# An embedding tower unrolled, with three one-tile gather buffers and nine tables looked up by matmul

## The reference

```python
e = jnp.stack([tbl_f[ids[:, f]] for f in range(26)], axis=1)      # [B, 26, 128], written out in full
combined = jnp.concatenate([dense[:, None, :], e], axis=1)         # [B, 27, 128]
inter = jnp.einsum('bfd,bgd->bfg', combined, combined)[:, TRIU_I, TRIU_J]   # 351 pairs
z = jnp.concatenate([dense, inter], axis=1)
h = jnp.concatenate([z, dense], axis=1)                            # [B, 607]
h = relu(h @ W_top1 + b_top1)                                      # 512
h = relu(h @ W_top2 + b_top2)                                      # 256
y = h @ W_top3                                                     # 1
```

## Time and profile before

| | us |
|---|---|
| median of 3 runs | 683.96 (681.14 to 686.35) |
| span of the profiled execution | 696.8 |
| PE busy / POOL busy / DVE busy / ACT busy in it | 377.1 / 312.2 / 209.2 / 92.9 |
| granted TensorE clock in it, mean | 0.740 of full speed |

### The profile page before, as it was taken

The page is one execution under the profiler, slowest core; times in us unless marked ns, Lnnn a source line. Parts: engine busy times, 40 slices in busy tenths (PEclk is TensorE's granted clock), DMA queues, the critical chain, the costliest instruction groups (busy, mean ns, idle before and its releaser), DMA issues.

```text
span 696.8 us, 13458 instructions
## 1 busy us (share of the span) xinstructions
PE 377.1 (54%) x5828; PEld 317.6 (46%) x5828; DVE 209.2 (30%) x561; ACT 92.9 (13%) x159; POOL 312.2 (45%) x308
## 2 busy tenths in 40 slices
PE   1306523396284843927349082771817547194897
PEld 1306422394174732717238071561716545083875
DVE  3524007140083100921029010461006600075121
ACT  1111000021011200202002020100201011011132
POOL 6770546304537054470736617174271733637100
PEclk9757755598588775977769595695858858588798
DMA  5651111111101111030101201012010200101000
GB/s 163 189 159 61 41 38 47 31 54 37 41 15 53 64 42 34 21 104 4 49 26 29 100 12 53 16 38 87 20 53 8 98 26 27 49 7 52 19 3 2
DMA packets 18087, 34.32 MB, mean 49 GB/s; under 512 B 8241, under 2 KB 10929, under 8 KB 18065
## 3 DMA queue, kind: packets, MB, share of 16 engines
q0 software_dynamic: 9728, 19.94, 10.0%
q1 hardware_dynamic: 8338, 14.06, 6.1%
HBM read 33.97 MB, written 0.01 MB: 49 GB/s over the span
## 4 chain that ended last, share of the span: by engine, by line
PE 47%; issue 29%; another core or an unknown queue 16%; DMA 4%; ACT 3%; DVE 1%; SPq 0%; ACTq 0%
PE flip_ps L306 15%; PE gram_ps L323 12%; PE flip_ps L290 6%; PE mlp_ps L348 6%; PE mlp_ps L357 5%; DMA raw_then_y<-tbl 4%; ACT feats L456 2%; PE mlp_ps L350 2%; PE mlp_ps L376 1%; ACT hi L619 1%; PE pairs_ps L336 0%; ACT xT L546 0%; ACT xT L549 0%; DVE dots L468 0%
## 5 line engine op out<-in xcount | busy, mean ns | idle before, releaser
L269 POOL DMA_INDIRECT emb<-tbl,idx x304 | 312.0, 1026 | 336.4 <-DMA idx<-ids 225.5
L306 PE MATMUL flip_ps<-marks,hi 125*128 125x256 f32 x448 | 129.6, 321 | 106.0 <-ACT feats L456 102.0
L323 PE MATMUL gram_ps<-feats 128*27 128x27 f32 x4096 | 86.2, 202 | 169.2 <-issue 165.6
L448 DVE COPY feats<-flip_ps 128x512 f32<-128x512 f32 x56 | 38.5, 688 | 400.8 <-remote 247.9
L323 PEld LDWEIGHTS gram_ps<-feats 128*27 128x27 f32 x4096 | 63.7, 113 | 200.1 <-issue 198.6
L306 PEld LDWEIGHTS flip_ps<-marks,hi 125*128 125x128 f32 x448 | 98.8, 220 | 110.9 <-issue 69.7
L484 DVE TENSOR_SCALAR marks<-id_cols,row_no 125x256 fp32r<-125x256 int32 x448 | 127.5, 362 | 32.8 <-remote 25.1
L306 PE MATMUL flip_ps<-marks,lo 125*128 125x256 f32 x448 | 124.6, 310 | 0.9 <-issue 0.9
L306 PEld LDWEIGHTS flip_ps<-marks,lo 125*128 125x128 f32 x448 | 98.7, 220 | 2.1 <-issue 1.8
L290 PE MATMUL flip_ps<-ident,emb 128*128 128x128 f32 x320 | 62.2, 320 | 31.2 <-issue 18.2
L456 ACT COPY feats<-flip_ps 128x512 f32<-128x512 f32 (+1 forms) x32 | 31.5, 984 | 237.0 <-remote 126.1
(11 more groups left out here) (23 smaller groups left out, 77.9 us busy)
## 6 DMA issues: line engine op xcount, KB each, us to landing
id_cols<-ids_in_pairs SPq DMA_DIRECT2D x8, 896.0 KB
emb<-tbl,idx POOLq DMA_INDIRECT x304
emb<-dense SPq DMA_DIRECT2D x16, 64.0 KB
raw_then_y<-tbl SPq DMA_DIRECT2D x2, 500.0 KB
dots<-tbl SPq DMA_DIRECT2D x2, 500.0 KB
h1T<-tbl SPq DMA_DIRECT2D x2, 500.0 KB
w1p_sb<-w_pairs SPq DMA_DIRECT2D x1, 702.0 KB
w_sb<-w SPq DMA_DIRECT2D x1, 512.0 KB
```

The lines of the kernel that those rows point to most:

```text
L269: nc.gpsimd.indirect_dma_start(emb[:, u, f, :], None, tables[order[f - 1]][:, :], bass.IndirectOffsetOnAxis(ap=idx[:, u, order[f - 1]:orde ...
L306: last = nc.tensor.matmul(flip_ps[:, m % 2, 2 * (s % 2):2 * (s % 2) + 2, :], part[s][0:R[s], c, :], marks[0:R[s], s % MARK_SLOTS, c, :], s ...
L323: last = nc.tensor.matmul(gram_ps[QUAD * j:QUAD * j + F, n, 0:F], row, row, start=True, stop=True)
L448: copy(feats[:, u, :, GROUP * k:GROUP * k + n], flip_ps[:, m % 2, 0:n, :].rearrange("d f p -> d p f")).then_inc(s_kept[m % 2], 1)
```

## The change

- The loops go: the program is written out for all 16 tiles.
- `LOOKED_UP` goes from 7 to 9 (two tables of 1,250 rows, also cut into 125 rows or fewer for each chunk, join the seven), so 17 tables are gathered for each tile. Marks and look-ups are handed over in half tables (4 chunks), with four half-table mark slots in place of four whole ones.
- `emb` has three slots of one tile. The gathers of tile t wait for the flips of tile t-3. The third slot serves as two of the waiting places of the raw tables at the start (five places now), so the gathers of tile 2 wait until all nine tables are split (`s_lo`).
- All ids are loaded at the start in two DMAs; `id_cols` is double-buffered. Tiles are now 128 consecutive samples. Each tile's outputs are stored by a DMA of their own.
- PE's order: a look-up group comes ahead of its flip, the third layer ahead of `pair_rows`, and the gram of both tiles is in quarters. ACT makes `hi` with looked-up groups between. DVE copies all flips of tile 0, ACT all of tile 1.

```diff
-LOOKED_UP = 7
+LOOKED_UP = 9
+SLOTS = 3
...
-        idx = sb("idx", [P, 2, TABLES], i32)
-        emb = sb("emb", [P, 2, GATHERED, P])
+        idx = sb("idx", [P, tiles, TABLES], i32)
+        emb = sb("emb", [P, SLOTS, GATHERED * P])
-        marks = sb("marks", [P, MARK_SLOTS, MAX_CHUNKS, 2 * P], fp32r)
+        marks = sb("marks", [P, MARK_SLOTS, HALF_CHUNKS, 2 * P], fp32r)
...
# SP, after the loads of tables and weights
-            with sp.Fori(1, pairs) as i:
-                sp.wait_ge(s_marked, LOOKED_UP * i)
-                load_columns(i)
-                for u in range(2):
-                    sp.wait_ge(s_flip, GROUPS * (2 * (i - 1) + u + 1))
-                    load_idx(i, u)
-                    load_dense(i, u)
+            sp.wait_ge(s_lo, LOOKED_UP)
+            load_dense(2)
+            for t in range(SLOTS, tiles):
+                sp.wait_ge(s_flip, GROUPS * (t - SLOTS + 1))
+                load_dense(t)
+                i = t // 2
+                if t % 2 and i + 1 < pairs:
+                    sp.wait_ge(s_marked, 2 * LOOKED_UP * i)
+                    load_columns(i + 1)
+                if t % 2 and i >= 2:
+                    store(2 * (i - 2), i - 2)
+                    store(2 * (i - 2) + 1, i - 2)
...
# POOL
-                    pool.wait_ge(s_idx[u], 16 * i + 16)
-                    if not first:
-                        pool.wait_ge(s_flip, GROUPS * (2 * (i - 1) + u + 1))
+            for t in range(tiles):
+                v = t % SLOTS
+                if t < 2:
+                    pool.wait_ge(s_idx[t], 16)
+                if t == SLOTS - 1:
+                    pool.wait_ge(s_lo, LOOKED_UP)
+                if t >= SLOTS:
+                    pool.wait_ge(s_flip, GROUPS * (t - SLOTS + 1))
...
# PE
+            def looking_up(i):
+                for k in range(GROUPS):
+                    look_up(i, k)
+                    if i and k == 0:
+                        pair_rows(2 * i - 1)
+                    flip(2 * i, k)
+                    if i and k:
+                        first_layer(i - 1, BOTH, 2 * (i - 1), range(k - 1, k))
+            for i in range(pairs):
+                looking_up(i)
+                for part in range(4):
+                    gram(2 * i, part)
+                    if part < 3:
+                        flip(2 * i + 1, part)
+                if i:
+                    second_layer(i - 1, BOTH)
+                flip(2 * i + 1, 3)
+                if i:
+                    third_layer(i - 1, BOTH)
+                pair_rows(2 * i)
+                if i == pairs - 1:
+                    first_layer(*LAST[0], 2 * i)
+                flip(2 * i + 1, 4)
+                for part in range(4):
+                    gram(2 * i + 1, part)
...
# DVE
+            for i in range(pairs):
+                if i:
+                    lay_out(2 * i - 1)
+                    dve.wait_ge(s_xT, 2 * (2 * i - 2) + 1)
+                mark_table(i, 2)
+                keep(2 * i, 0)
+                mark_table(i, 3)
+                mark_table(i, 4)
+                keep(2 * i, 1)
+                mark_table(i, 5)
+                mark_table(i, 6)
+                keep(2 * i, 2)
+                mark_table(i, 7)
+                mark_table(i, 8)
+                keep(2 * i, 3)
+                keep(2 * i, 4)
...
+                if i + 1 < pairs:
+                    mark(i + 1, 0)
+                lay_out(2 * i)
+                if i + 1 < pairs:
+                    mark(i + 1, 1)
+                    mark_table(i + 1, 1)
...
# ACT, at the start
             for s in range(LOOKED_UP):
                 act.wait_ge(s_raw[s % PLACES], 16 * (s // PLACES + 1))
                 nc.scalar.copy(hi[s][0:R[s], :, :], waiting(s)).then_inc(s_hi, 1)
+                if s >= 4 and s % 2 == 0:
+                    keep_looked(0, s // 2 - 2)
```

## The result

The changed kernel took 721.96 us (718.81 to 724.28, 4 runs) against 682.55 us (678.57 to 686.35, 4 runs): 1.057 times as long, with an interval of 1.051 to 1.063. The forecast was 711, slower, within 655 to 733.

The account below looks back on a forecast made before the run. Bound: PE shut out during POOL's gather runs. Period 24.4 + 10.2 + 24.4 + 30.7 = 89.7 us against 84.1; with start and end a 724 us span, times 0.982: 711 us, slower, range 655 to 733.

Parts of the forecast that it names:

- The shut stretches: After each tile's last flip, POOL's gather run leaves PE almost no instructions until 3.5 us after it: 24.4 us each.
- no shutting out: Rival: PE isn't shut out at all, loops or slots written while read were behind it; about 460 us, chance 0.06.
- Stretch 2 loses its cover: Tile 1's gram, before passing while marks held the first gather, is caught in the run: full 24.4 us, 160 matmuls left.
- The paragraph on ids: Ids loaded once: POOL starts at the flip, 2.6 us sooner; PE does that work behind the stretch, worth nothing by itself.
- The rule on the port: GpSimd can't write DMA descriptors while VectorE takes both ports; by it alone, half-table marks would give the cover back.
- Two more tables: PE's look-ups: 16 matmuls a table, 1.89 us, so 3.8 us a pair, all on PE's path.
- The open stretches: PE's time between the runs of a pair: 10.2 us after the first, 30.7 us with the look-ups after the second.
- Third slot and ids: Slot covers nothing in steady state, only moves one run from end to start; loading ids once is worth nothing by itself.
- Start and end: Pair 1's first trigger at 174 us against 160.4 before; pair 6's at 622.5, then gram and look-ups run free; span 724.
- From span to time: Timed median taken as 0.982 of the profiled span, so a span of 724 us gives 711 us.

Follow-up runs that it names:

- e10: Changed kernel with the gathers of tiles 3 to 15 replaced by same-size plain copies issued by SP: 462.39 us, kernel before 701.6 on that chip.
- e7: Changed kernel with the gathers of tiles 4, 6, ... 14 waiting for the gram of tile t-3, not its last flip: 687.46 us, 0.985 of kernel before.
- e8: Kernel before with its loops written out and all ids loaded once at the start, nothing else: 699.79 us, 1.001 of the kernel before.
- e4: Same kernel as e7, on the chip where the kernel before takes 425.31 us: 456.99 us, 1.077 times the kernel before.
- e9: Changed kernel with both tiles' gathers started together after both grams of a pair, one run of 34: 713.46 us, 1.019 of the kernel before.
- e1: Changed kernel without the gathers of tiles 3 to 15, on the chip where the kernel before takes 425.31 us: 452.88 us.
- e3: Same kernel as e10, on the chip where the kernel before takes 425.31 us: 432.95 us.

## Why the prediction was right, and where it wasn't

- *The shut stretches.* Right, in both grams. They last 24.0 us (264.47 to 288.47 and 299.47 to 323.50), said were 24.4. 17 gathers are 20.9 us, as worked out. That POOL's gathers are the cause, and neither the amount of traffic nor the loops, is shown by e10 and, for the loops, by the changed kernel itself. Why a gather should stop PE isn't shown, and the rule holds on some chips only: on the one with 425 us the forecast's whole mechanism is absent. I had taken one chip's trace for the kernel's behaviour. That the result was taken on a chip with the shutting out is luck as far as the forecast goes: its 6% for no shutting out stood for causes in the kernel, not for another chip.
- *Stretch 2 loses its cover.* Right, and the heart of the loss: e7 gives the gram free passage in another way and wins some 6 us a pair, more than the 4.7 that were lost (88.8 less 84.1). In one half it stays open. The prediction named two parents of the cover, POOL's wait for ids and the marks. e8 removes the first and keeps the cover, so loading the ids once didn't lose it as long as the marks stayed where they were. No run moved the marks and kept the wait for the ids, which might have let a part of the gram through. The paragraph on ids fits e8 in its own sum (worth nothing).
- *The rule on the port.* The Trainium skill, "SBUF — State Buffer", section on the two separate sides, fits e8 (7.19 us beside marks that end 0.8 us earlier) as it fitted the 4.16 us; the 1.03 us of pair 0 remains against it, and so do the seven gathers behind it, 0.94 or 0.95 us each beside the same row of marks (to 117.34), and the first gather at 122.13 in the result's trace, 0.99 us beside marks that run from 120.91 to 125.27. Whether these marks run in a mode that takes both ports no row shows.
- *Two more tables.* Mis-sized. The rows of the smaller tables gave 16 matmuls for each, but the two new ones have 10 chunks: 40 matmuls a pair and not 32, 4.7 us and not 3.8.
- *The open stretches.* 11.0 us (288.47 to 299.47) for 10.2, and 29.8 (323.50 to 353.26) for 30.7. With the shut ones the period is 88.8 us, for 89.7.
- *Third slot and ids.* No gain from either appears: in steady state PE waits for no gathered data, and POOL waits 14 and 33 us for flips in each pair.
- *Start and end.* The nine tables were split at 64.6 (said 67), both runs ran in a row until 108.5, and pair 1's first trigger was at 175.87 (said 174). Pair 6's was at 619.51 (said 622.5) with 103.0 us behind it (said 101.5). The span came to 722.5 us, said 724.
- *From span to time.* This is the 11 us of the miss: I scaled by 0.982, as the first profile stood to its timed runs. Here the profiled execution, 722.5 us of span, took 724.28 us by the clock of the timed runs. If the same 1.8 us belong to the 696.8 us of the first profile, it was of an execution of 698.6 us, longer than any of the timed runs beside it. The kernel before spreads by 2% on one chip and by 3% between the chips on which PE is shut out.

## What to carry to other kernels

Before removing waits ahead of a burst of DMA issues, look at what passes in their shelter: here marks on another engine held a gather for a few microseconds, a gram of 256 matmuls slipped through, and a change that took this shelter away cost more than the fewer gathers brought. Where a run of software gathers disturbs another engine, start it behind the instruction-dense stage and lay it over the sparse one, in several short runs. And measure both kernels on more than one chip before believing a mechanism: on one of those met here it didn't exist.

## What the hardware showed that I had not expected

**One chip without the shutting out.** The same kernel before takes 425 us on one chip, 699 to 703 on three others, and 683 in the result's runs. The granted clock doesn't explain it; PE is idle, not slow, in the windows above. What sets the one chip apart stays open.

**Written-out code pauses in fast bursts.** The loop of the kernel before fetched no instructions from 205 to 615 us; the changed kernel does, in the same window of its trace:

```profile
q8 instruction: 28, 0.46, 0.5%
q14 instruction: 5, 0.04, 0.0%
```

In a gram that isn't shut out the unrolled kernels then show a pause of microseconds. The loop doesn't: behind the 187 matmuls of the earlier trace rows the other 69 follow after 0.44 us, and the jump shows 0.42. In e4, where no stretch is shut, it is:

```profile
227.15 0.30 PE L311 MATMUL gram_ps<-feats 128*27 128x27 f32 x8 [4.28 <-issue]
...
240.27 1.28 PE L311 MATMUL gram_ps<-feats 128*27 128x27 f32 x108 [1.53 <-issue]
```

and in e9 at the same places:

```profile
359.33 0.26 PE L309 MATMUL gram_ps<-feats 128*27 128x27 f32 x8 [3.91 <-issue]
```

In e1, without gathers, it is 3.38 us at this place. In e10 the first of the two is 0.62 us (191.01, again 8 matmuls); there SP issues the load of `id_cols`, 1152 KB, at 195.75, behind this pause and ahead of the second, which is then 2.90 us (to 203.34). In e1, e4 and e9 it issues it 4.4 to 4.5 us ahead of the first pause (in e4 at 218.38), and the load takes 6.6 us to land, so that the pause begins while it is under way. And in the last two pairs of e4, for which no such load is left, the first pause is 1.00 and 1.22 us, after 3.59 to 4.28 in the five pairs before. So fetches that queue behind a large load are the likely reason, which was not tried by itself. The two pauses together make 3.5 (e10) to 6.4 us (e9) a pair, which the shut stretches of the changed kernel hide in part. They are also a part of what sets e3 apart from e1 on the same chip, 432.95 us with SP's copies and 452.88 with none: PE's idle time for "issue" ahead of gram matmuls is 30.8 us in e3 and 42.4 in e1. The Trainium skill ("Runtime: NRT & Kernel Launch", on instruction fetch mechanics) prefers full unrolling; at these places the loop was the better one, though e8, written out, is no slower than the kernel before as a whole (1.001).
